# Attention with a quantised feed-forward on one core: sharing out the extra work of steps 0 to 14 otherwise

## The reference

```python
kv_c = x @ W_kv_down                       # rank 64
k_rope = rope(kv_c @ W_k_rope)             # 4 key heads x 64
q = concat(q_nope, rope(q_rope))           # 16 heads x 192
attn = softmax(causal(q @ k.T * scale)) @ v
out = attn @ W_o

qx = round(x / sx); sx = max|x| / 127                  # one scale for all
qw = round(w / sw); sw = max|w| / 127 per row of w
h = gelu((qx @ qw1.T) * (sx * sw1) + b1)               # 256 -> 1024
y = quantised(h) @ qw2.T * scales + b2                 # 1024 -> 256
```

## Time and profile before

| what | value |
|---|---|
| median of 3 runs | 638.79 us (633.93 to 644.43) |
| the profiled execution | 633.81 us |
| its span in the profile | 632.0 us |
| what lies around the span | 1.8 us |
| mean granted TensorE clock | 0.97 |
| step 0 begins (first maxima) | 68.28 us |
| step 16 begins | 344.4 us |
| PE, DVE, ACT, POOL busy in the span | 569.6, 528.4, 458.8, 459.5 us |

### The profile page before, as it was taken

The page is one execution under the profiler, slowest core; times in us unless marked ns, Lnnn a source line. Parts: engine busy times, 40 slices in busy tenths (PEclk is TensorE's granted clock), DMA queues, the critical chain, the costliest instruction groups (busy, mean ns, idle before and its releaser), DMA issues.

```text
span 632.0 us, 15802 instructions
## 1 busy us (share of the span) xinstructions
PE 569.6 (90%) x6298; PEld 413.9 (65%) x6298; DVE 528.4 (84%) x825; ACT 458.8 (73%) x713; POOL 459.5 (73%) x258
## 2 busy tenths in 40 slices
PE   7888986878989999999999989898999999988896
PEld 5556454556667666666677667676776767767475
DVE  5988678875897888888888889898888889898896
ACT  3546563887887677877788878787878888867962
POOL 3258866987688389948998878888888887770146
PEclk9879887999999899999999999999999999999999
DMA  8863795889899999999999999999999998999403
GB/s 244 268 205 94 224 179 120 135 149 180 163 189 191 173 167 173 169 175 187 162 173 161 162 161 174 189 171 187 154 180 142 173 153 163 158 158 162 90 1 134
DMA packets 323657, 104.15 MB, mean 165 GB/s; under 512 B 305856, under 2 KB 316672, under 8 KB 323456
## 3 DMA queue, kind: packets, MB, share of 16 engines
q1 hardware_dynamic: 320112, 97.82, 84.7%
q10 hardware_dynamic: 3472, 5.31, 3.1%
HBM read 19.21 MB, written 8.39 MB: 44 GB/s over the span
## 4 chain that ended last, share of the span: by engine, by line
PE 44%; DVE 20%; DMA 16%; ACT 7%; POOL 5%; issue 5%; SPq 2%; DVEq 0%; POOLq 0%; ACTq 0%
PE psum L1183 41%; DMA pt<-p_src 14%; DVE small L996 5%; DVE p_src L1004 3%; ACT psum L734 3%; DVE small L1119 3%; SPq L416 2%; ACT p_src L728 2%; POOL res L586 1%; PE psum L1400 1%; DVE bnst L832 1%; DVE acc L844 1%; POOL q_raw L530 1%; DMA acc<-in_L_attn_x 1%; POOL q_swap L524 1%
## 5 line engine op out<-in xcount | busy, mean ns | idle before, releaser
L728 ACT ACTIVATE p_src<-psum,small 128x1024 f16<-128x1024 f32 (+7 forms) x256 | 184.0, 744 | 114.1 <-DVE small L996 113.8
L996 DVE TENSOR_REDUCE small<-psum 128x1 f32<-128x1024 f32 (+7 forms) x256 | 186.6, 749 | 45.4 <-PE psum L1183 44.9
L1004 DVE TENSOR_TENSOR p_src<-psum,p_src 128x1024 f16<-128x1024 f32 (+2 forms) x192 | 182.5, 951 | 28.2 <-ACT psum L734 26.6
L734 ACT ACTIVATE psum<-psum,small 128x1024 f32<-128x1024 f32 (+7 forms) x256 | 179.0, 722 | 0.0
L1183 PE MATMUL psum<-kv_tok,pt 128*128 128x65 f16 (+1 forms) x3456 | 138.3, 193 | 22.5 <-DMA pt<-p_src 17.0
L1183 PEld LDWEIGHTS psum<-kv_tok,pt 128*128 128x128 f16 x3456 | 122.9, 98 | 49.3 <-issue 27.0
L1183 PE MATMUL psum<-k_hi,q_hi 128*128 128x512 f16 (+3 forms) x384 | 125.7, 331 | 13.3 <-POOL q_lo L539 5.1
L1183 PE MATMUL psum<-k_lo,q_hi 128*128 128x512 f16 (+3 forms) x384 | 126.5, 330 | 0.0
L1183 PE MATMUL psum<-k_hi,q_lo 128*128 128x512 f16 (+3 forms) x384 | 126.5, 330 | 0.0
L521 POOL TENSOR_TENSOR q_swap<-q_raw,sin_sb 32x1024 f32<-32x1024 f32 x32 | 75.2, 2350 | 55.4 <-ACT q_raw L663 54.7
L530 POOL TENSOR_TENSOR q_raw<-q_raw,q_swap 64x1024 f32<-64x1024 f32 x32 | 76.1, 2377 | 2.5
(11 more groups left out here) (173 smaller groups left out, 862.2 us busy)
## 6 DMA issues: line engine op xcount, KB each, us to landing
pt<-p_src SPq DMA_TRANSPOSE x288, 3.8
acc<-in_L_attn_x SPq DMA_DIRECT2D x8, 512.0 KB, 5.6
wq_split<-w_split SPq DMA_DIRECT2D x4, 1024.0 KB, 5.0
wq<-wq_split ACTq DMA_DIRECT2D x12, 256.0 KB, 3.1
ffn_t<-in_L_attn_W_o SPq DMA_DIRECT2D x1, 2048.0 KB, 19.6
k_rotated<-k_split SPq DMA_DIRECT2D x8, 256.0 KB, 2.6
w_sb<-in_L_ffn_w SPq DMA_DIRECT2D x2, 1024.0 KB, 7.5
out_x<-res SPq DMA_DIRECT2D x8, 256.0 KB, 2.2
```

What stands on the lines that cost most here:

```text
L728: ins = act.activation(p_src[u][:, 0, at:at + w], psum[:, COLS[i]:COLS[i] + w], ACT.Exp, bias=nb)
L734: ins = act.activation(ps, ps, ACT.Exp, bias=nb)
L996: dve.tensor_reduce(sm["mcol"][:, NT * (n % 2) + i:NT * (n % 2) + i + 1], psum[:, COLS[i]:COLS[i] + (i + 1) * P], AX.X, ALU.max, negate=True)\
L1004: dve.tensor_tensor(p_src[u][:, 1, :], psum[:, o:o + WIDE[u]], p_src[u][:, 0, :], ALU.subtract)\
```

## The change

1. `EXTRA` is rewritten for steps 3 to 14. Turned integers: before, `w` 0 and 1 in step 2, `x` 0, `w` 2, `x` 2, `w` 3 in step 3, the other six `x` in step 4; now `w` 0 and 1 in step 2, `w` 2 in step 3, `w` 3 and three `x` in step 4, one `x` in step 5, four `x` in step 6. Key products: before, steps 7, 8, 11 and 12 with units 3 and 5; now the even steps 8, 10, 12 and 14 with units 2 and 5.
2. The three reloads of tokens that stood behind unit 3 of steps 5, 6 and 7 stand behind unit 3 of steps 6, 7 and 8; each waits that its own tiles have been turned.
3. The weight maxima are taken in four pieces: five rows per partition of w1 at the end of step 0, the other three behind unit 0 of step 1, the first row of w2 behind unit 1 and the second behind unit 3 of step 1.
4. The sine product of `kb` is written back to its PSUM bank instead of `kt_b`, and added from there to `kt_a`. What ScalarE waits for follows.

```diff
 EXTRA = {0: [(0, "ka", 2), (2, "kb", 2)],
          1: [(0, "kv", 1)],
          2: [(0, "ka", 3), (2, "kb", 3), (3, "w", 0), (5, "w", 1)],
-         3: [(1, "x", 0), (3, "w", 2), (4, "x", 2), (5, "w", 3)],
-         4: [(0, "x", 1), (1, "x", 4), (2, "x", 3), (3, "x", 5), (4, "x", 6), (5, "x", 7)],
-         7: [(3, "ka", 4), (5, "kb", 4)], 8: [(3, "ka", 5), (5, "kb", 5)],
-         11: [(3, "ka", 6), (5, "kb", 6)], 12: [(3, "ka", 7), (5, "kb", 7)]}
+         3: [(4, "w", 2)],
+         4: [(0, "w", 3), (2, "x", 2), (3, "x", 3), (5, "x", 0)],
+         5: [(4, "x", 1)],
+         6: [(0, "x", 6), (2, "x", 7), (3, "x", 4), (5, "x", 5)],
+         8: [(2, "ka", 4), (5, "kb", 4)], 10: [(2, "ka", 5), (5, "kb", 5)],
+         12: [(2, "ka", 6), (5, "kb", 6)], 14: [(2, "ka", 7), (5, "kb", 7)]}
+LARGEST_AT = {(0, 5): (0, 0, 5), (1, 0): (0, 5, 8), (1, 1): (1, 0, 1), (1, 3): (1, 1, 2)}
...
             def reload_x(i):
                 t = 4 * RELOADED[i]
+                sp.wait_ge(S["misc_full"], X_TURNED[2 * RELOADED[i] + 1] + 1)
                 sp.dma_start(acc[:, t:t + 4, :], x_tok[:, t:t + 4, :]).then_inc(acc_in[i], 16)
...
-                        if u == 3 and 5 <= n < 8:
-                            reload_x(n - 4)
+                        if u == 3 and 6 <= n < 9:
+                            reload_x(n - 5)
                     if n == 4:
-                        sp.wait_ge(S["misc_full"], misc_index(4, "x", 7) + 1)
                         reload_x(0)
...
-            def weight_largest(k):
+            def weight_largest(k, first, end):
...
+                largest_of, w = sm[name][:, c], (w1_sb if k == 0 else w2_sb)[:, c, :]
+                chained(dve.tensor_reduce(largest_of, w, AX.X, ALU.max, apply_absolute_value=True))
+                chained(dve.tensor_scalar(largest_of, largest_of, 1.0 / QMAX, Q_EPS, ALU.mult, ALU.max))
                 if k == 0:
-                    dve.tensor_scalar(sm["s1"], sm["w1s"], sm["sx"], None, ALU.mult)
-                chained(dve.reciprocal(sm["r" + name], sm[name]))
-                dve.sem_inc(S["w_scaled"], 1)
+                    dve.tensor_scalar(sm["s1"][:, c], largest_of, sm["sx"], None, ALU.mult)
+                chained(dve.reciprocal(sm["r" + name][:, c], largest_of))
+                if end == (D // P if k else INNER // P):
+                    dve.sem_inc(S["w_scaled"], 1)
...
-                    dve.wait_ge(S["kr_sum"], n)
-                    dve.tensor_tensor(kt_b[:, :], misc_bank(idx), sin_sb[:, cb], ALU.mult).then_inc(misc_used(idx), 1)
-                    dve.wait_ge(misc_used(idx), USERS_AHEAD[idx] + 1)
-                    dve.tensor_tensor(kt_a[0][:, :], kt_a[0][:, :], kt_b[:, :], ALU.add).then_inc(S["kr_sum"], 1)
+                    chained(dve.tensor_tensor(misc_bank(idx), misc_bank(idx), sin_sb[:, cb], ALU.mult))
+                    dve.tensor_tensor(kt_a[0][:, :], misc_bank(idx), kt_a[0][:, :], ALU.add).then_inc(misc_used(idx), 1)
```

More of the change, by code:

```diff
@@ L129 @@
 ONE_BANK = MISC_BASE + sum(n == 0 for n, _, _ in MISC_AT)
+KEYS_TURNED = {k: MISC_BASE + i for (_, kind, k), i in MISC_AT.items() if kind == "kb"}
+X_TURNED = {k: MISC_BASE + i for (_, kind, k), i in MISC_AT.items() if kind == "x"}
 BANK_OF = [7 if i < ONE_BANK else 6 + i % 2 for i in range(MISC_END)] + [4, 5]
@@ L655, in keys_high @@
                     act.wait_ge(kr_stored[0], 16 * (n - 1))
-                act.wait_ge(S["kr_sum"], n + 1)
+                if n < 2:
+                    act.wait_ge(S["kr_sum"], n + 1)
+                else:
+                    summed = KEYS_TURNED[n]
+                    act.wait_ge(misc_used(summed), USERS_AHEAD[summed] + 1)
                 act.activation(k_split[i][:, 0, :], kt_a[i][:, :], ACT.Copy).then_inc(S["kr_hi"], 1)
@@ L1046, in latents_low @@
                                          kv_tok[:, 8 * k:8 * k + 8, 0:LAT], ALU.subtract)
-            def weight_largest(k):
+            def weight_largest(k, first, end):
                 dve.wait_ge(S["w2_in" if k else "w1_in"], 16)
-                name = "w1s" if k == 0 else "w2s"
-                chained(dve.tensor_reduce(sm[name], w1_sb if k == 0 else w2_sb, AX.X, ALU.max, apply_absolute_value=True))
-                chained(dve.tensor_scalar(sm[name], sm[name], 1.0 / QMAX, Q_EPS, ALU.mult, ALU.max))
+                name, c = "w1s" if k == 0 else "w2s", slice(first, end)
+                largest_of, w = sm[name][:, c], (w1_sb if k == 0 else w2_sb)[:, c, :]
+                chained(dve.tensor_reduce(largest_of, w, AX.X, ALU.max, apply_absolute_value=True))
+                chained(dve.tensor_scalar(largest_of, largest_of, 1.0 / QMAX, Q_EPS, ALU.mult, ALU.max))
                 if k == 0:
-                    dve.tensor_scalar(sm["s1"], sm["w1s"], sm["sx"], None, ALU.mult)
-                chained(dve.reciprocal(sm["r" + name], sm[name]))
-                dve.sem_inc(S["w_scaled"], 1)
+                    dve.tensor_scalar(sm["s1"][:, c], largest_of, sm["sx"], None, ALU.mult)
+                chained(dve.reciprocal(sm["r" + name][:, c], largest_of))
+                if end == (D // P if k else INNER // P):
+                    dve.sem_inc(S["w_scaled"], 1)
             def wvo_low(k):
@@ L1095, in _ @@
                         latents_low(0, bank[5]).then_inc(S["kvt_lo"], 1)
-                    if (n, j) in ((1, 1), (1, 4)):
-                        weight_largest(j // 4)
+                    if (n, j) in LARGEST_AT:
+                        weight_largest(*LARGEST_AT[n, j])
                     if (n, j) == (1, 1):
```

## The result

The changed kernel is slower: 646.0 us median (640.51 to 651.59) beside 639.08 for the kernel before, timed with it, a ratio of 1.0086 with a 95% interval of 1.0056 to 1.0117. That is +5.5 us (3.6 to 7.5) where -1.8 was forecast. It lies within the 2% that I gave 0.88, but on the other side of zero and beyond the range's upper end of 644.

A forecast was written before the change was run, and what follows sets the result against it. TensorE was taken to bound most steps; VectorE, the key reload or GpSimd limited some long ones. Terms -0.7 - 0.3 + 0.5 + 0.1 - 2.4 + 1.0 = -1.8 us gave 637.0 us, 8-in-10 range 626 to 644.

The forecast's parts named there:

- the 2% that I gave 0.88: Whole kernel: a change within 2%, 12.8 us, about what a measurement can tell; faster 0.07 and slower 0.05 were left.
- the same GpSimd order: Steps 10 to 15: each odd step held by kb at unit 5, keys_low, then rotation, at 16.35 us.
- +1.0: Steps 10 to 15: three pairs of key products instead of two, 95.85 us against 94.86 before.
- my 15.6: Each even step of steps 10 to 15: 14.1 us plus 1.5 for both key products.
- The bound of +3: Steps 10 to 15: upper bound, if a store of keys costs another transpose wait.
- that bound: Steps 7 to 9, forecast -2.4 us: from -5.5 without reload waits to +4.4 if the reloads collide.
- the rival of colliding reloads: Steps 7 to 9: each reload costs 1.8 us waiting and 1.7 by clock; total +5.0, 643.8 us; chance 0.17.
- the range's lower end: Whole kernel: 626 us, given as the spread in full with steps 7 to 9 at their lower bound.
- the spread in full: Rival at step 4: it starts 5.0 us earlier and no clock is lost; total -7.8, 631 us; chance 0.25.
- not five: Start of step 4: 0.7 us earlier, not five, because the keys' second load still sets it.
- The rival of the lock: Steps 2 to 4: reciprocals wait for GpSimd too, moving them 1.5 us further; total -0.3, 638.5 us; chance 0.13.
- the sum at 0.7 us: Step 2: kb's sum from PSUM never waits for GpSimd, saving VectorE 1.8 us, counted as nothing in the total.

The follow-up runs named there:

- kb_early: The changed kernel with the key products at units 0 and 2 of steps 8, 10, 12 and 14 instead of 2 and 5: 637.93 us, ratio 0.9973.
- load_early: The changed kernel with step 3's key store and first key load moved ahead of and behind the first unit's transposes on SyncE: 641.71 us, ratio 1.0044.
- load_before: The kernel before with step 3's key store ahead of the first unit's transposes on SyncE and the key reloads directly behind them: 636.11 us, ratio 0.9985.
- gp_order: The changed kernel with GpSimd rounding keys of steps 8 and 12 behind the next query's split, their store one step later: 640.29 us, ratio 1.0010.
- keys_only: The kernel before with only the key products moved, to units 2 and 5 of steps 8, 10, 12 and 14: 646.98 us, ratio 1.0120.
- sum_back: The changed kernel with kb's sine product written to kt_b in SBUF again and the sum taken from there: 645.72 us, ratio 1.0046.
- maxima_back: The changed kernel with the weight maxima again in two pieces, behind units 1 and 4 of step 1: 643.09 us, ratio 1.0056.

## Why the prediction was wrong

**The step that failed** is "Each odd step after it is held by the same GpSimd order, `kb` at unit 5, `keys_low`, rotation, so 16.35", and with it "+1.0" for steps 10 to 15. The mechanism was right, and TensorE waits for q_lo where I said; its size was not. I took 16.35 for the price of the order, but it was read from a step that itself began late (a 0.94 us wait for an earlier query), because before, two key products stood in neighbouring steps and the second one's hand-over lay partly in the first one's delay. Without that lateness it would have been 17.3, and so would step 13 of the kernel before, 15.94 us after a start 1.34 late. Spaced out, every odd step pays in full. The half us from 17.3 to 17.8 lies in the hand-over: ScalarE's copy of the keys starts 2.64 us behind the end of step 10's product, and started 2.21 behind that of step 8 before; why is open. By TensorE's first scores the six steps add up so: odd steps 17.79, 17.76 and 17.78 instead of 16.35, +4.3; even steps 15.34 without a clock drop, close to my 15.6, so -0.8; and the drop behind two of the waits 16.97 + 16.81 - 2 x 15.34 = +3.1, for which I had counted nothing. Together +6.6, the whole of 102.5 against 95.85. The bound of +3 was too near as well, and step 9, 17.95 instead of 16.6, is the same error once more (17.35 by first scores; the rest are step 10's first scores at half clock).

**Also wrong, and smaller.** Step 7 with its reload took 15.75, not 17.5, and step 8 18.18, not 16.5; it is luck that the two together missed by only 0.1. Steps 7 to 9 came out 1.3 longer than forecast through step 9. Neither end of that bound was reached, so the rival of colliding reloads was not what made the change slower: kb_early keeps the reloads, and has 48.39 us there. Steps 5 and 6 cost +1.5 where I counted +0.6: step 5 with its one `x` took 1.0 more, not 0.5, and step 6 with its four, and without the reload, 0.5 more, not 0.1; why is open. And the range's lower end was added up wrongly: the spread in full with steps 7 to 9 at their lower bound gives -10.9, which is 628 us; 626 needs steps 10 to 15 at their lower bound too.

**Right.** The end of step 3 was held by the second load, not by TensorE: 4.37 us of idle (4.5 forecast) ended by `k_lo`, and the clock at half rate behind it; steps 0 to 4 gave 1.4 us where 1.0 was forecast, and "not five" (in the four profiles with all of the change's early parts and the late load they took 96.3 to 97.7 us, in the two with neither changed 97.6 and 98.0). With that the rival "spread in full" fell for the reason given against it, and load_early and load_before showed it by lifting the queue's order; even so load_early's steps 0 to 4, at 93.62, are 4.0 us shorter than before, not the 7.0 of that rival. VectorE's products of over 2 us, the sum at 0.7 us and the 1.0 us that steps 0 and 1 together cost (43.47 against 42.45) came as worked out. The rival of the lock is not borne out: step 2 began as forecast without it, and the reciprocal at 106.55 took 0.16 us beside a busy GpSimd. But that one has a single column, and the two larger ones, at 97.34 and 103.08, began just as a GpSimd instruction ended, so whether a reciprocal of several columns waits is not shown.

On the clock, the Trainium skill ("TensorE: Matmul & The Clock Gate", Part 1) says that an idle array falls back to half rate. It held behind the wait ahead of step 4 (granted 0.50) and behind three of the four q_lo waits (0.51 to 0.56), and in the sum I had weighed it at step 4 only; three drops of 1.5 us in steps 10 to 16 would have turned the forecast's sign. The wait of 2.66 us at 320.49 that no drop followed shows that such a wait does not always bring one; what decides between the two stays open here.

## What to carry to other kernels

A floor read from a step that itself began late is too low: take the chain's own length (here 14.3 us from hand-over to first scores) and ask when it would start if nothing before it were late. Extra work at the end of a step brought no wait here where its consumer, an engine in program order, had nothing due behind it; so move it to an earlier unit, or put the due work ahead of it. And price a new wait of TensorE with the half-clock stretch that can follow it.

## What the runs showed of the hardware

Waits of 1.9 to 2.7 us of TensorE for q_lo were followed by a stretch at a granted clock near 0.5 in three of four cases of the kernel after and in neither of two in gp_order; in keys_only, load_early, sum_back and maxima_back, with four such waits of 1.7 to 2.7 us each, in three, three, two and two. So the same wait cost some 1.5 us more, or nothing.

The exclusion of VectorE and GpSimd worked both ways here, and by who came first: a sum from SBUF of 0.69 us, begun in the gap between two GpSimd instructions, made the second last 2.83 instead of 2.37 us, while the same sum begun behind GpSimd's start lasted 2.45. That agrees with the Trainium skill ("SBUF — State Buffer", SBUF: two separate sides), which has whichever starts first hold the ports for its whole instruction.
